# A residual add moved to TensorE and a rounding to ScalarE in the middle stage of a five-engine tower

## What is computed

```python
def layer_norm(x, g, b):
    mu = jnp.mean(x, axis=-1, keepdims=True)
    var = jnp.mean((x - mu) ** 2, axis=-1, keepdims=True)
    return (x - mu) * jax.lax.rsqrt(var + EPS) * g + b

def quantum_circuit(v):
    return jnp.cumprod(jnp.cos(v), axis=-1)
...
attn_out = quantum_circuit(xh).reshape(B, T, C)      # xh: heads of 16
x1 = layer_norm(x + attn_out, gamma1, beta1)
q = quantum_circuit(x1[..., :nq])                    # nq = 16
h = jnp.einsum('btq,fq->btf', q, w1) + b1
ffn_out = jnp.einsum('btf,cf->btc', jax.nn.relu(h), w2) + b2
return layer_norm(x1 + ffn_out, gamma2, beta2)
```

## Time and profile before

| | us |
|---|---|
| median of the runs | 1659.44 |
| the profiled execution, whole | 1659.89 |
| its span | 1658.20 |
| busy: TensorE, VectorE, GpSimd, ScalarE | 1313.6, 962.8, 745.5, 504.5 |
| `middle`, from its first to its last instruction | 923 to 1318 |

### The profile page before, as it was taken

How to read it: one execution, slowest core, us unless ns; L and a number is a source line. 1 busy time by engine, 2 the same in 40 slices (tenths; PEclk the granted TensorE clock), 3 DMA queues, 4 the chain that set the end, 5 groups by cost and what they waited for, 6 DMA issues and landing times. The chain is left out here.

```text
span 1658.2 us, 23461 instructions
## 1 busy us (share of the span) xinstructions
PE 1313.6 (79%) x6824; PEld 912.0 (55%) x6824; DVE 962.8 (58%) x2728; ACT 504.5 (30%) x966; POOL 745.5 (45%) x936
## 2 busy tenths in 40 slices
PE   1267878877899839999999267777777489999997
PEld 0245555545666426666666155555555357776665
DVE  7565775776666544444444468888886424444443
ACT  1024444434555412222222234344433111111111
POOL 2552353535121234455444456656564335444553
PEclk9968788889989669999999677777777689999999
DMA  6447346444857241211121532221100181110000
GB/s 155 79 77 114 71 91 134 87 65 102 150 132 138 69 167 57 65 64 63 65 64 40 161 117 93 81 82 57 58 7 13 32 312 30 33 31 28 28 25 11
DMA packets 97449, 134.69 MB, mean 81 GB/s; under 512 B 18208, under 2 KB 80302, under 8 KB 96304
## 3 DMA queue, kind: packets, MB, share of 16 engines
q1 hardware_dynamic: 77536, 93.52, 24.3%
q0 software_dynamic: 16416, 38.46, 7.4%
q10 hardware_dynamic: 3376, 1.22, 0.4%
HBM read 75.43 MB, written 35.73 MB: 67 GB/s over the span
## 5 line engine op out<-in xcount | busy, mean ns | idle before, releaser
L966 DVE TENSOR_REDUCE top_a_a<-s_bank 128x4 f32<-128x1024 f32 x128 | 156.5, 1223 | 110.7 <-PE s_bank L616 107.3
L1506 PE MATMUL mbank<-w2T_m,fhT_m 128*128 128x256 f32 x512 | 154.6, 468 | 0.0
L792 ACT ACTIVATE prob_a<-s_bank 128x1024 f32<-128x1024 f32 x128 | 130.4, 1019 | 77.1 <-PE s_bank L637 75.4
L1935 PE MATMUL ebank<-w,exT 128*128 x312 | 142.5, 600 | 0.7 <-ACT exT L1981 0.7
L1946 PE MATMUL ebank<-w,ehT 128*128 x624 | 141.2, 379 | 0.9 <-ACT ehT L1989 0.9
L1506 PEld LDWEIGHTS mbank<-w2T_m,fhT_m 128*128 128x128 f32 x512 | 120.0, 241 | 37.3 <-ACT fhT_m L1620 10.2
L1163 PE MATMUL ebank<-w,exT 128*128 x284 | 135.5, 600 | 0.6 <-ACT exT L1210 0.6
L1175 PE MATMUL ebank<-w,ehT 128*128 x568 | 134.4, 380 | 0.8 <-ACT ehT L1216 0.8
L1122 POOL DMA_INDIRECT ex<-rows_d,tile_row x71 | 72.8, 1026 | 120.2 <-DVE sent_to L1248 102.2
L1946 PEld LDWEIGHTS ebank<-w,ehT 128*128 128x128 f32 x624 | 115.6, 190 | 15.7 <-issue 1.6
L527 POOL DMA_INDIRECT rows_d<-h_a,row_i_a x64 | 63.7, 995 | 129.9 <-DVE row_i_a L1052 115.0
(11 more groups left out here) (342 smaller groups left out, 2669.9 us busy)
## 6 DMA issues: line engine op xcount, KB each, us to landing
w<-in_L_ffn_W SPq DMA_DIRECT2D x16, 1024.0 KB, 10.0
qs_a<-parts_q_a SPq DMA_DIRECT2D x96, 128.0 KB, 4.4
ks_a<-parts_k_a SPq DMA_DIRECT2D x96, 128.0 KB, 6.4
w<-in_L_ffn_w SPq DMA_DIRECT2D x16, 512.0 KB, 5.2
image_a<-in_x SPq DMA_DIRECT2D x4, 1024.0 KB, 7.6
h_d<-rec_a SPq DMA_DIRECT2D x4, 1024.0 KB, 3.8
x_a<-h_d SPq DMA_DIRECT2D x16, 256.0 KB, 3.2
h_d<-h_a SPq DMA_DIRECT2D x16, 256.0 KB, 2.5
```

What stands on the lines that cost most here:

```text
L792: nc.scalar.activation(prob[:, j % 4].rearrange("p g t s -> p (g t s)"), s2_bank[:].rearrange("p g s -> p (g s)"), ACT.Exp, scale=HD ** -0 ...
L966: nc.vector.tensor_reduce(top[:, j].rearrange("p g t -> p (g t)"), s1_bank[:].rearrange("p g (t s) -> p (g t) s", t=TPI), axis=AX, op=ALU. ...
L1506: last = nc.tensor.matmul(b[:, t * D:(t + 1) * D], hT[:, f, t * P:(t + 1) * P], w2T[:, f, :], start=False, stop=f == FC - 1)
L1935: last = nc.tensor.matmul(bank[1 + n % 2][:], xT[j % 2][:, ch, :], w[:, bass.ds(e, 1), at:at + 512].rearrange("p a f -> p (a f)"), start=c ...
```

## The change

In `middle`: the residual `x1g` is added in F2 by a matmul of the identity with `x1g`, into the same bank; R2 then takes its statistics directly from the bank, B2 reads the bank too, and `r2` is gone. The constant row is split into two rows (0 and 32 of a tile of 33 rows, zeros between) of the single-pass operand type, and multiplied once. The turns are rounded by two activations of ScalarE, behind `h2` and ahead of `x1`; VectorE does `r1` in one operation in RTa, and GpSimd's `r1` is gone. GpSimd's A0 comes behind the scatter and B2 instead of first in the turn; `x1g` stands later in the list. In D and R one copy each is saved (`pick` and `rank`). At the stage's start VectorE has some more fills and, in `prep`, three more small operations. In `attention`: the six fills of `ks` go from VectorE to GpSimd, behind its other fills and each with a wait for its end.

```diff
@@ attention, GpSimd @@
+            for u in range(RING):
+                for half in (32, 96):
+                    c.link(nc.gpsimd.memset(ks[u][half:half + 32].bitcast(F32), 1.0))
+            pool.sem_inc(q["ks_ok"], 2 * RING)
             pool.wait_ge(q["w_in"], 16 * 4)
@@ attention, VectorE @@
             weigh_rest(0, last=False)
-            for u in range(RING):
-                for half in (32, 96):
-                    nc.vector.memset(ks[u][half:half + 32].bitcast(F32), 1.0).then_inc(q["ks_ok"], 1)
@@ middle, order @@
-        STEPS = [("load", "n2"), ("A0", "n1"), ("A1", "n"), ("root0", "n"), ("h2", "n"), ("SC", "m"), ("root1", "m"), ("RTa", "n"), ("r1", "n"), ("x1", "m"),
-                 ("T", "p"), ("XQ", "m"), ("x1g", "m"), ("qsin", "m"), ("D", "p"), ("rk", "p"), ("RTb", "n"), ("sin", "n"), ("prep", "n"),
-                 ("SQa", "m"), ("qc", "m"), ("R2", "f"), ("root2", "f"), ("SQb", "m"), ("F1", "m"), ("R", "p"), ("scatter", "p"),
-                 ("B2", "f"), ("root3", "f"), ("h2b", "n"), ("F2", "m"), ("h3", "f")]
+        STEPS = [("load", "n2"), ("A1", "n"), ("root0", "n"), ("h2", "n"), ("SC", "m"), ("root1", "m"), ("RTa", "n"), ("x1", "m"),
+                 ("T", "p"), ("XQ", "m"), ("qsin", "m"), ("D", "p"), ("rk", "p"), ("RTb", "n"), ("sin", "n"), ("prep", "n"),
+                 ("SQa", "m"), ("qc", "m"), ("x1g", "m"), ("R2", "f"), ("root2", "f"), ("SQb", "m"), ("F1", "m"), ("R", "p"), ("scatter", "p"),
+                 ("B2", "f"), ("A0", "n1"), ("root3", "f"), ("h2b", "n"), ("F2", "m"), ("h3", "f")]
@@ middle, GpSimd @@
-            def r1(i):
-                pool.wait_ge(q["n_ok"], i + 1)
-                if i >= 1:
-                    pool.wait_ge(q["arg_ok"], i)
-                nc.gpsimd.tensor_tensor(r1_[:], turns_[:], flat(h2[i % 2]), ALU.add).then_inc(q["r1_ok"], 1)
@@ middle, TensorE, F2 @@
-                    nc.tensor.matmul(b[:, t * D:(t + 1) * D], ones_f[0:1, :], shift1[0:1, :], start=True, stop=False)
+                    nc.tensor.matmul(b[:, t * D:(t + 1) * D], ones_r[0:33, :], shift_hl[0:33, :], start=True, stop=False)
+                    if t == 0:
+                        pe.wait_ge(q["x1g_ok"], i + 1)
+                    nc.tensor.matmul(b[:, t * D:(t + 1) * D], ident[:], x1g[i % 2][:, t, :], start=False, stop=False)
@@ middle, ScalarE, behind h2 @@
+                act.wait_ge(q["h2_ok"], i + 1)
...
+                nc.scalar.activation(turns_[:], flat(h2[i % 2]), ACT.Identity, bias=magic[:, 0:1], scale=INV).then_inc(q["t_ok"], 1)
+                act.wait_ge(q["t_ok"], i + 1)
+                nc.scalar.activation(turns_[:], turns_[:], ACT.Identity, bias=off_magic[:, 0:1]).then_inc(q["n_ok"], 1)
@@ middle, VectorE, prep @@
-                    nc.vector.tensor_tensor(shift1[:], be1[:], b2[:], ALU.add).then_inc(q["w_ok"], 1)
+                    c.link(nc.vector.tensor_tensor(shift1[:], be1[:], b2[:], ALU.add))
+                    c.run(nc.vector.tensor_copy(shift_hl[0:1, :], shift1[0:1, :]))
+                    c.link(nc.vector.tensor_copy(shift_hi[32:33, :], shift1[32:33, :]))
+                    nc.vector.tensor_tensor(shift_hl[32:33, :], shift1[32:33, :], shift_hi[32:33, :].bitcast(F32), ALU.subtract).then_inc(q["w_ok"], 1)
@@ middle, VectorE, RTa and RTb @@
-                dve.wait_ge(q["h2_ok"], i + 1)
-                c.link(nc.vector.tensor_scalar(turns_[:], flat(h2[i % 2]), INV, MAGIC, ALU.mult, ALU.add))
-                nc.vector.tensor_scalar(turns_[:], turns_[:], -MAGIC, -C1, ALU.add, ALU.mult).then_inc(q["n_ok"], 1)
+                dve.wait_ge(q["n_ok"], i + 1)
+                nc.vector.scalar_tensor_tensor(out=r1_[:], in0=turns_[:], scalar=-C1, in1=flat(h2[i % 2]), op0=ALU.mult, op1=ALU.add)\
+                    .then_inc(q["r1_ok"], 1)
...
-                nc.vector.scalar_tensor_tensor(out=arg[:], in0=turns_[:], scalar=C21, in1=r1_[:], op0=ALU.mult, op1=ALU.add)\
+                nc.vector.scalar_tensor_tensor(out=arg[:], in0=turns_[:], scalar=-C2, in1=r1_[:], op0=ALU.mult, op1=ALU.add)\
@@ middle, VectorE, R2 and B2 @@
-                nc.vector.tensor_tensor(flat(r2), bank[4 + i % 2][:], flat(x1g[i % 2]), ALU.add).then_inc(q["r2_ok"], 1)
-                dve.wait_ge(q["r2_ok"], i + 1)
-                variances(2, r2)
+                variances(2, bank[4 + i % 2][:].rearrange("p (t d) -> p t d", t=TPI))
...
-                    ins = nc.vector.scalar_tensor_tensor(out=z2[:, t, :], in0=r2[:, t, :], scalar=moments[2][:, t, 0:1], in1=g2[:],
+                    ins = nc.vector.scalar_tensor_tensor(out=z2[:, t, :], in0=bank[4 + i % 2][:, t * D:(t + 1) * D], scalar=moments[2][:, t, 0:1], in1=g2[:],
@@ middle, VectorE, D and R @@
-                c.link(nc.vector.tensor_tensor(pick[:], iota8[:].unsqueeze(1).to_broadcast([P, TPI, E]),
-                                               idx_f[:].to_broadcast([P, TPI, E]), ALU.is_equal))
-                nc.vector.tensor_copy(both[:], pick[:]).then_inc(q["pick_ok"], 1)
+                nc.vector.tensor_tensor(both[:], iota8[:].unsqueeze(1).to_broadcast([P, TPI, E]),
+                                        idx_f[:].to_broadcast([P, TPI, E]), ALU.is_equal).then_inc(q["pick_ok"], 1)
...
-                c.link(nc.vector.tensor_copy(rank1[:, TPI * i:TPI * i + TPI], rank_f[:, :, 0]))
```

More of the change, by code:

```diff
@@ L1301, in middle @@
         hT = sb("fhT", [P, FC, SEQ])
-        sum_, sum2, r2, z2, r3 = (sb(n, [P, TPI, D]) for n in ("sum_", "sum2", "r2", "z2", "r3"))
+        sum_, sum2, z2, r3 = (sb(n, [P, TPI, D]) for n in ("sum_", "sum2", "z2", "r3"))
         h2 = [sb(f"h2_{u}", [P, TPI, D]) for u in range(2)]
@@ L1432, in x1g_ @@
                 if i >= 2:
-                    pool.wait_ge(q["r2_ok"], i - 1)
+                    pool.wait_ge(q["f2_ps"], i - 1)
                 nc.gpsimd.tensor_tensor(x1g[i % 2][:], x1[:], g1[:].unsqueeze(1).to_broadcast([P, TPI, D]), ALU.mult).then_inc(q["x1g_ok"], 1)
@@ L1454, in _ @@
                    "root1": lambda i: root(i, 1), "root2": lambda i: root(i, 2), "root3": lambda i: root(i, 3),
-                   "r1": r1, "x1g": x1g_, "h2b": h2b_, "scatter": scatter})
+                   "x1g": x1g_, "h2b": h2b_, "scatter": scatter})
             c.reset()
@@ L1783, in R @@
                 nc.vector.tensor_tensor(cnt[:], bank[7][:, TPI * E:(TPI + 1) * E], cnt[:], ALU.add).then_inc(q["rk_ok"], 1)
[L1784 to L1786 removed]
+                c.link(nc.vector.tensor_tensor(prod[:], both[:], rk[:], ALU.mult))
+                ranks = rank1[:, TPI * i:TPI * i + TPI]
+                c.link(nc.vector.tensor_reduce(ranks, prod[:], axis=AX, op=ALU.add))
+                nc.vector.scalar_tensor_tensor(out=row_i[i % 2][:, :, 0], in0=idx_f[:, :, 0], scalar=float(SLOTS), in1=ranks,
                                                op0=ALU.mult, op1=ALU.add).then_inc(q["row_ok"], 1)
[L1788 removed]
                 dve.wait_ge(q["rk_ok"], i + 1)
```

32 lines of the change are left out of this document (17 added, 15 removed).

## The result

The changed kernel took **1649.26 us** (median of 5 runs, 1646.75 to 1652.63); the kernel before, run beside it, 1661.4 (1659.33 to 1664.88). The ratio is 0.9927, with a 95% interval of 0.9906 to 0.9948: 12.1 us or 0.73% faster. The forecast was 1651.0, 8.5 us faster; the time lies inside its range, and the gain is 1.4 times what was forecast. The profiled execution's span went from 1658.2 to 1644.9 us, 13.3 less.

What follows compares the result with a forecast made beforehand. Two loops of waits, equally long in the turn read, set a middle turn: VectorE-GpSimd-ScalarE and TensorE. Start -6.1, twelve full turns 0, three others -2.4, together -8.5: forecast 1651.0 us, range 1644 to 1658.5.

Steps and rivals of the forecast that it cites:

- The fills: Start, attention: with the `ks` fills on GpSimd, VectorE's sums begin at 25.3 and TensorE's at 33.1 instead of 39.23, -6.1 us.
- A0 behind the scatter: Middle turn: GpSimd's add of `hin` now delays `sum_`, 3.85 to 3.9 after the first scatter instead of 2.75, +1.13 us.
- Root 0 earlier: Middle turn: root 0 finds GpSimd free, so `h2` starts 1.65 after `sum2` instead of 2.83, -1.18 us.
- Rival one: Middle: A0's 1.13 is paid each turn but root 0 isn't earlier, +1.2 a turn, 1666.5 us; chance 0.09.
- The rounding: Middle turn: two ScalarE activations between `h2` and `x1` cost 1.33, less 0.61 that `x1` waits anyway, +0.72 us.
- Loop one: Middle turn: the loop of waits over VectorE, GpSimd and ScalarE; its terms sum to +0.02 us a turn.
- The residual: Middle: VectorE's saved add is worth nothing in steady turns, as a wait replaces it; -0.7 us in each of three turns.
- F2, +0.1: Middle, TensorE: the single-pass constant row plus the residual's identity product change F2 by -0.2 to +0.3, taken as +0.1 us.
- Rival three: Middle: the turn shrinks too, about 0.3 us a turn, as loop two binds in most turns; 1645 us, chance 0.22.
- loop two: Middle turn: the loop of waits over TensorE, from F2 through its logits to D; changes by -0.1 us a turn.
- The other turns: Middle: three turns, the first after F2 begins and the last two, change by 3 x (-0.7 - 0.2 + 0.1) = -2.4 us.
- Smaller ones: Middle: direct `rank`, four more fills and three `prep` operations (0.3 each) cost nothing; without cover by `arg`, `prep` costs +1.

Runs made afterwards that it cites:

- fills_only: The kernel before with only the fills of `ks` moved from VectorE to GpSimd; ratio 0.9965 to the kernel before, 1650.26 us.
- a0_first: The changed kernel with GpSimd's add A0 put back to the head of the turn, ahead of root 0; ratio 0.9918 to the kernel before, 1643.43 us.
- turns_on_vector: The changed kernel with the rounding of the turns put back from ScalarE to VectorE; ratio 0.9905 to the kernel before, 1637.67 us.
- add_on_vector: The changed kernel with the residual added by VectorE into `r2` again, without the identity's products; ratio 0.9924 to the kernel before, 1644.68 us.
- fills_and_row: The kernel before with the `ks` fills on GpSimd and the constant row in a single pass; ratio 0.9942 to the kernel before, 1645.19 us.
- scan_pool_add_vector: The changed kernel with second scan and its copies earlier, A0 behind `x1g`, `h2b` behind root 1, residual on VectorE; ratio 0.9824 to the kernel before, 1626.89 us.

## Why the prediction was right, and where it was off

In short: the time lies in the range because the start, half of the gain, came as forecast and for the reason given; for the rest the width of the range did its part. In the middle the sign was right and the source was not: the forecast gave the steady turns nothing and took its 2.4 us from the first and the last turns, mostly for the residual. The runs show the constant row instead, which alone takes 7.6 us from the stage, and which the sum held, together with the residual's products, at +0.1 a turn.

**The fills, -6.1.** Right, and for the reason given: -6.03 at the transposes, 5.8 us by the times of fills_only. The sums began at 24.50 (forecast 25.3) and the fills ended at 27.04 (28.5). One thing was missed: TensorE's sum waited 0.69 for ScalarE's copy `wT_o` behind the queued transposes, which made it 33.40 instead of 33.1.

**A0 behind the scatter, +1.13.** From the first scatter to `sum_` it is now 3.72 instead of 2.75, +0.97. The mechanism isn't that of the forecast, which had VectorE idle before `sum_`. VectorE's `minus`, two numbers per partition, starts 0.01 after A0 and ends 0.04 after it, 1.30 for what took 0.17. The Trainium skill tells this (SBUF — State Buffer, "SBUF: two separate sides"): VectorE in a two-port mode and GpSimd share a pair of ports under an exclusive lock, and whoever starts first holds it for its whole instruction. The trace agrees with the 1.30.

**Root 0 earlier, -1.18.** `h2` starts 1.64 after `sum2`, before 2.83: -1.19. With A0's +0.97 this gives -0.2, and a0_first, which undoes both, is no slower than the changed kernel. Rival one, which took this gain for doubtful, is out. The forecast left one thing out: before, A0 ran beside `sum2` and held it (1.57 in the earlier trace rows), now `sum2` takes 0.69, and root 1 behind it ends 3.3 after `sum2`'s start instead of 4.4.

**The rounding, +0.72.** The start of `h2` to that of `x1` went from 1.70 to 2.51, +0.81; an activation took 0.72, not the 0.63 read from one without a tile for its bias. The Trainium skill has the difference (ScalarE: Activation LUTs, "What ACT_TABLE_LOAD costs"): a bias from a tile adds a fixed part, by its formula an estimated 0.71 for 512 elements. The trace agrees, with 0.72. A second point was missed: once `h2` comes 1.19 earlier, `x1` meets root 1, so without the rounding it would have gained only part of that. The edit's price is 0.35, as turns_on_vector shows.

**`r1` removed, -0.45, and the cast, -0.20.** XQ's second operation starts 0.26 after `x1`'s end instead of 0.66, -0.40; from the copy of the logits to `arg` it is 1.25 instead of 1.48, -0.23.

**Loop one, +0.02.** The plain turn went from 21.48 to 21.36, -0.12. By add_on_vector (21.56) this is +0.08 from these edits and -0.20 from the residual, which the forecast had at nothing here.

**The residual, nothing in steady turns.** Right in the net and in the wait that replaced it (0.83 before SQb). Put back on VectorE the add costs 0.20 in a plain turn, not nothing, but the shorter F2 pays for it. The -0.7 in each of the last two turns isn't seen: from the last `sum_` to `last_experts` add_on_vector takes 72.8 and the changed kernel 73.5. The Trainium skill's objection to a source in PSUM (VectorE: DVE Perf Modes, "The TRN2 errata"), an estimated 0.26 a turn, isn't borne out: 24 statistics took 410 ns each (median) from PSUM and 418 from SBUF, and `z2`'s operation 480 from PSUM where it took 486 from SBUF before.

**F2, +0.1: the term that was mis-sized.** As a whole F2 came out at -0.20 by the eleven of the table and at -0.12 over a whole round, inside what was given, near its lower end. The row gave -1.0 (11.28 to 10.31, and 12.16 to 11.15) where the forecast allowed it 0.5 to 0.8, and the identity costs +0.8. Then the sum said that the longer loop sets a turn and took the turn's change for 0, although show that TensorE's loop set five of the thirteen. The row alone takes the mean turn from 21.78 to 21.50, as the turns that waited for the logits become plain ones; the other edits without the residual bring it to 21.57 and the residual to 21.61. Against the kernel before that is -0.20, 12 turns, -2.4 us, of which -0.12 stands in every plain turn. Rival three had named F2's -0.2, but its loop two was to bind most turns, and it binds four of the twelve. The forecast's lower end of -4 for this term held it.

**The other turns, -2.4.** They gave -4 to -5. Up to the fourth `sum_` the trace of before has 48.40 us from the first, fills_only, with the same code in the middle, 47.79, and the changed kernel 46.13. From the last `sum_` to the end it is 412.98, 412.59 and 410.28. With the row alone (fills_and_row) it is 408.24, so the last turns' part needs none of the other edits. Which part of this is the clock's (the third turn took 22.28 and 21.00 us in the two executions of the same code) stays open.

**Smaller ones.** The three operations more in `prep` took 1.0 us and weren't covered: `sum_` of the second image starts right behind them (1.53 after the start of the operation ahead of them, before 0.34). That turn is shorter all the same (9.66 for 10.61), since GpSimd's adds no longer run beside `arg` (1.74 before, 0.69 now) and the first cast of `prep` (1.29 and 0.22). The more fills at the stage's start are three, not four.

**The sum.** Start -5.8, steady turns -2.4, the others -4 to -5: -12 to -13, against 12.1 in the times and 13.3 in the spans.

## What to carry to other kernels

Where two loops are nearly equal, price an edit in both, and count the turns that each sets; a term in a loop that sets only some of the turns gave the middle's whole gain here, and the edits that looked large cancelled. An edit that frees an engine ahead of a wait is worth nothing until the wait is moved: find who the wait is for, and whether what it waits for could be made sooner (one swap in the order gave about as much as the change). In a part that starts on a slow clock, the time of an instruction is not its price: what is added ahead of others may cost less than it takes, since the others then run fast.

## What the runs showed of the hardware

**TensorE's clock follows the turn, and then holds it.** From the second steady turn to the last the granted clock of every kernel here stood at 2.4 GHz for 10.2 us each time and at 1.2 GHz for 10.2 or 13.6. In four kernels whose loops were short enough the turn closed in on 20.48 us, from above in one and from below in three; that the clock holds it there is my reading. The Trainium skill describes a matmul kernel that falls back to the slow clock in every iteration (TensorE: Matmul & The Clock Gate, "HAM oscillation — how this bites in real kernels"); the rows agree that the slow clock comes back each turn. That a pipeline settles on the clock's own rhythm wasn't expected.

**Executions of the same code differ ahead of the middle.** With the fills moved, the code up to the middle is the same in the changed kernel and in all twelve others, but in their executions, on several chips, the middle's first fill began between 911.15 and 917.48 us. A change in one stage has to be read from inside that stage, and a single span can mislead by some us: fills_and_row's span is 10.8 us under that of fills_only, its stage 7.6.

**The order of two engines decides who pays.** Beside VectorE's `minus`, GpSimd's add of 512 elements took 1.27 us and VectorE 1.30 for 0.17. In scan_pool_add_vector the same add starts 0.08 behind `arg`, and there GpSimd pays: its add took 1.72, and `arg` with 0.67 lost nothing.

```profile
1104.00 0.67 DVE L1701 SCALAR_TENSOR_TENSOR arg_m<-turnsn_m,rest_m 128x512 f32<-128x512 f32 x1
1104.08 1.72 POOL L1417 TENSOR_TENSOR hin_m<-hin_m,ya_m 128x512 f32<-128x512 f32 x1 [4.00 <-DVE both_m L1787]
```
